# The adapter's four batches rewritten as one stream of 23 slots

## The reference, cut to what matters

```python
enc, ca = ctx[:, :73], ctx[:, 73:]                  # 77 rows of 96; the last 4 are tokens
hs      = mha(x @ Wq, enc @ Wk, enc @ Wv)           # text branch, 8 heads of 20
ca_q1   = einsum('btc,th->bch', ca, Wq_ca)[:, indices]   # 96 distinct rows, repeated to 512
ca_hs1  = mha(ca_q1, x, x)                          # token branch: softmax over 512 rows of x
ca_hs2  = mha(ca_hs1 @ Wq, ca @ Wk_ca, ca @ Wv_ca)  # softmax over 4 tokens
x       = (hs + ca_hs2) @ Wout + b_out + x
```

## Time and profile before

| | |
|---|---|
| runs | 1092.45, 1094.27, 1095.04 us; median 1094.27 |
| profiled execution, span | 1096.6 us, 2.3 over the median |
| PE, DVE, ACT, POOL busy | 93%, 64%, 55%, 32% of the span |
| mean granted TensorE clock | 0.964 |
| adapter | from 0 to about 215 us |

### The profile page before, as it was taken

One profiled execution on the slowest core, in us unless ns is written; L12 is line 12 of the kernel. 1 busy time (PEld: TensorE's weight loads), 2 busy tenths in 40 slices (PEclk: granted clock), 3 DMA queues, 4 the chain that ended last, 5 costly groups with the idle time before them and its releaser, 6 DMA issues.

```text
span 1096.6 us, 17611 instructions
## 1 busy us (share of the span) xinstructions
PE 1018.4 (93%) x6388; PEld 721.8 (66%) x6388; DVE 706.5 (64%) x1228; ACT 598.1 (55%) x1344; POOL 350.0 (32%) x461
## 2 busy tenths in 40 slices
PE   6788887799999999999999999999999989999998
PEld 3455553556666766666766666766656569999887
DVE  2544737377767467767367767377662879999563
ACT  2534434466677456677366676366662654555432
POOL 2303214133433224433233433133331023444220
PEclk9878988899999999999999999999999999999999
DMA  6700000000000000000000000000000240000000
GB/s 165 186 1 1 2 1 0 1 1 1 1 1 1 1 1 2 1 1 1 1 1 1 1 1 1 1 1 1 1 1 1 64 129 14 1 1 1 1 25 25
DMA packets 25319, 17.67 MB, mean 16 GB/s; under 512 B 8482, under 2 KB 24050, under 8 KB 25234
## 3 DMA queue, kind: packets, MB, share of 16 engines
q1 hardware_dynamic: 25234, 16.54, 5.8%
HBM read 11.29 MB, written 1.31 MB: 11 GB/s over the span
## 4 chain that ended last, share of the span: by engine, by line
PE 61%; DVE 10%; ACT 5%; issue 4%; POOL 1%; DMA 0%; SPq 0%; DVEq 0%; ACTq 0%; POOLq 0%
PE banks L415 12%; PE banks L402 11%; PE banks L388 10%; PE banks L422 4%; ACT sa_probs L505 3%; PE banks L224 3%; PE banks L226 2%; PE banks L227 2%; PE banks L225 2%; PE banks L1460 2%; PE banks L1752 2%; DVE sa_negmax L577 2%; DVE ca_top L1595 1%; DVE ca_probs L1600 1%; PE banks L232 1%
## 5 line engine op out<-in xcount | busy, mean ns | idle before, releaser
L645 POOL TENSOR_SCALAR sa_probs<-sa_probs,sa_inverse 128x512 f32<-128x512 f32 x320 | 217.6, 696 | 373.8 <-DVE sa_inverse L581 373.7
L505 ACT ACTIVATE sa_probs<-banks,sa_negmax 128x512 f32<-128x512 f32 x320 | 215.9, 685 | 163.2 <-DVE sa_negmax L577 163.1
L577 DVE TENSOR_REDUCE sa_negmax<-banks 128x2 f32<-128x1024 f32 x160 | 188.6, 1218 | 12.6 <-PE banks L388 9.9
L402 PE MATMUL banks<-ident,sa_probs 128*128 128x128 f32 x1280 | 175.1, 278 | 10.0 <-ACT sa_turned L516 5.7
L402 PEld LDWEIGHTS banks<-ident,sa_probs 128*128 128x128 f32 x1280 | 146.9, 142 | 55.9 <-issue 28.0
L586 DVE COPY sa_turned<-banks 128x512 f32<-128x512 f32 x160 | 110.1, 688 | 77.5 <-PE banks L402 77.5
L415 PE MATMUL banks<-sa_turned,sa_v 128*64 128x512 f32 x640 | 155.0, 605 | 0.0
L388 PE MATMUL banks<-sa_k_parts,sa_q_parts 64*128 64x512 f32 x960 | 134.4, 411 | 1.9 <-ACT sa_probs L505 1.9
L516 ACT COPY sa_turned<-banks 128x512 f32<-128x512 f32 x160 | 94.4, 590 | 31.7 <-PE banks L402 30.0
L388 PEld LDWEIGHTS banks<-sa_k_parts,sa_q_parts 64*128 64x128 f32 x960 | 84.8, 187 | 31.2 <-issue 14.6
L415 PEld LDWEIGHTS banks<-sa_turned,sa_v 128*64 128x64 f32 x640 | 38.7, 136 | 74.2 <-issue 73.0
(11 more groups left out here) (212 smaller groups left out, 1757.4 us busy)
## 6 DMA issues: line engine op xcount, KB each, us to landing
w_o<-in_L_xattn_wo SPq DMA_DIRECT2D x2, 800.0 KB, 6.4
out<-x SPq DMA_DIRECT2D x4, 320.0 KB, 2.4
w_q_t<-in_L_xattn_wq_t SPq DMA_DIRECT2D x1, 1120.0 KB, 11.2
fold_values<-ca_turned SPq DMA_DIRECT2D x5, 192.5 KB
x<-in_x SPq DMA_DIRECT2D x1, 960.0 KB, 6.0
fold_values<-ca_probs SPq DMA_DIRECT2D x4, 192.5 KB
ad_raw_main<-in_L_xattn_wq SPq DMA_DIRECT2D x1, 640.0 KB, 4.1
ad_raw_main<-in_L_xattn_wk SPq DMA_DIRECT2D x1, 640.0 KB, 6.2
```

The costliest lines, as they stand in the source:

```text
L402: last = pe.transpose(b_turn[e][:, q * P:(q + 1) * P], probs[:, j % 2, e, q, k * P:(k + 1) * P], ident[:])
L505: act.activation(probs[:, j % 2, e, q, :], b_scores[u % 2][:, e, :], ACT.Exp, bias=negmax[:, u % RING, e:e + 1], accum_out=total[:, u % RI ...
L577: dve.tensor_reduce(negmax[:, u % RING, :], b_scores[u % 2], AX_X, ALU.max, negate=True).then_inc(s_max.sem, 1)
L645: pool.tensor_scalar(probs[:, j % 2, e, q, :], probs[:, j % 2, e, q, :], inverse[:, u % RING, e:e + 1], 1.0, ALU.mult, ALU.mult).then_inc( ...
```

## The change

The batch loop becomes a loop over 23 slots. Slot s has head pair s of the token branch (16 of them, batch s // 4) and query tile u = s - 4 of the text branch. A tile's probabilities are turned one slot after its scores, its products follow two slots after, and its projection and update of x three slots after. The batch's token tail (second query projection, four-token scores and softmax, expansion) is spread over slots 4b+4 to 4b+6, so that it is there when tile 0 of that batch is projected.

- All transposes, the query projections, the expansion and one extra product share two PSUM banks (2 and 3) in a fixed order (`Turns`): each filling waits for the copy of the filling two before. Which engine copies is fixed by item.
- Contexts of all four batches are loaded by one DMA (and tokens by one), and their token queries, keys and values are projected ahead of slot 0. Keys are spread into block-diagonal form by POOL with a mask, two batches' buffers deep, in place of DVE copies.
- The token values are multiplied by `wo` once (`token_outputs`, slot 2). Each tile's projection then has a third matmul, of the expanded probabilities (K = 32) with these folded values, and the accumulation onto all heads (L975) is gone.
- Products, their copy, the projection and the update of one tile use one bank (4).
- The weight splits are cut into 12 chunks, one in each of slots 3 to 14. The raw buffers lie over tiles that are loaded only later: the five large loads (`last`, 3.68 MB) are issued after the last chunk's remainder.
- x_pad, x_t and q_t get a second buffer; x_pad is cleared by DVE instead of POOL.

What follows is the new code's core; the helpers that are left out do the same operations on the same shapes as before, one tile or head pair at a time.

```diff
-class Raw:
-    def __init__(self, ctx, nc, name):
-        self.main = ctx.enter_context(nc.sbuf_tensor(name + "main", [P, INNER], F32))
-        self.tail = ctx.enter_context(nc.sbuf_tensor(name + "tail", [3 * DT, INNER], F32))
...
+class Turns:
+    BANKS = (2, 3)
...
+    def of_slot(s, units, delta):
+        b, k = divmod(s, QT)
+        u = s - delta
+        out = [("x", 0, g) for g in range(G)] if s == 0 else []
+        out += [("probs1", s - 1, e) for e in range(2)] if 1 <= s <= units else []
+        out += [("probs", u - 1, g) for g in range(G)] if 1 <= u <= units else []
+        if k == 0 and b < B:
+            out += [("queries", b, 0)]
+        if k == 1 and b + 1 < B:
+            out += [("x", b + 1, 0)]
+        if k == 2 and 1 <= b <= B:
+            out += [("expanded", b - 1, 0)]
+        if k == 2 and b == 0:
+            out += [("token_outputs", 0, 0)]
+        if k == 2 and b + 1 < B:
+            out += [("x", b + 1, 1)]
+        if k == 3 and b < B:
+            out += [("queries", b, 1)]
+        return out
...
+        return banks[Turns.BANKS[self.items.index(item) % 2]]
+    def wait_free(self, pe, item):
+        n = self.items.index(item) - 2
...
+def adapter(nc, t, x, ident, ctx_t, banks, splits, raws, later, last, next_ln):
...
+        NU = B * QT
+        DELTA = 4
+        SLOTS = NU + DELTA + 3
+        HT = H0 * NCA
...
+        b_s1, b_small, b_token, b_out = banks.pair(0), banks.pair(5), banks[7], banks[4]
...
+            def project_out(u):
+                b, q = divmod(u, QT)
+                rows = slice(b * HT, (b + 1) * HT)
+                pe.wait_ge(s_heads.sem, s_heads.at(u, 0))
+                if q == 0:
+                    ring.wait_copied(pe, ("expanded", b, 0))
+                for g in range(G):
+                    pe.matmul(b_out[:, OUT:OUT + D], heads[:, u % 2, g, :], wo[:, g, :], start=(g == 0), stop=False)
+                pe.matmul(b_out[:, OUT:OUT + D], probs2x[rows, q * P:(q + 1) * P], v2_out[rows, :], start=False, stop=True).then_inc(s_o.sem, 1)
...
+            for s in range(SLOTS):
+                b, k = divmod(s, QT)
+                u = s - DELTA
+                if s < NU:
+                    scores1(s)
+                if 1 <= s <= NU:
+                    turn_probs1(s - 1, 0)
+                    turn_probs1(s - 1, 1)
+                if k == 1 and 1 <= b <= B:
+                    project_hs1(b - 1)
+                if 0 <= u - 3 < NU:
+                    project_out(u - 3)
+                if 0 <= u < NU:
+                    scores(u)
+                if 0 <= u - 1 < NU:
+                    turn_probs(u - 1, 0)
+                    turn_probs(u - 1, 1)
+                if 0 <= u - 2 < NU:
+                    products(u - 2)
+                if k == 0 and b < B:
+                    project_queries(b, 0)
+                if k == 0 and 1 <= b <= B:
+                    products1(b - 1, 1)
+                if k == 1 and b + 1 < B:
+                    turn_x(b + 1, 0)
+                if k == 1 and 1 <= b <= B:
+                    scores2(b - 1)
+                if k == 2 and 1 <= b <= B:
+                    expand_probs2(b - 1)
+                if s == 2:
+                    token_outputs()
+                if k == 2 and b + 1 < B:
+                    turn_x(b + 1, 1)
+                if k == 2 and b < B:
+                    products1(b, 0)
+                if k == 3 and b < B:
+                    project_queries(b, 1)
+                if s == NU + 1:
+                    pe.wait_ge(s_exp1.sem, s_exp1.at(NU - 1, 1))
+                    next_ln.turn(pe, 0, ident, banks[0:2], lambda i: None)
...
+            for s in range(SLOTS):
+                b, k = divmod(s, QT)
+                u = s - DELTA
+                if 0 <= u - 3 < NU:
+                    copy_heads(u - 3)
+                if k == 1 and 1 <= b <= B:
+                    copy_hs1(b - 1)
+                if 1 <= s <= NU:
+                    copy_turned1(s - 1, 0)
+                    copy_turned1(s - 1, 1)
+                if k == 2 and 1 <= b <= B:
+                    exp2(b - 1)
+                if s < NU:
+                    exp1(s, 0)
+                    exp1(s, 1)
+                if k == 1 and 1 <= b <= B:
+                    copy_q2(b - 1)
+                if 0 <= u - 1 < NU:
+                    copy_turned(u - 1)
+                if 0 <= u < NU:
+                    exp(u)
+                if s in chunks:
+                    i, c = chunks[s]
+                    act.wait_ge(s_raw, 16 * Split.LOADS * len(splits))
+                    splits[i][1].round(act, raws[i], columns(c), s_rounded.sem)
+                if k == 0 and b < B:
+                    copy_queries(b, 0)
+                if k == 1 and b + 1 < B:
+                    copy_x(b + 1)
+                if k == 2 and 1 <= b <= B:
+                    copy_expanded(b - 1)
+                if s == 2:
+                    item = ("token_outputs", 0, 0)
+                    ring.wait_made(act, item)
+                    act.copy(v2_out[:], ring.bank(banks, item)[:, 0:D]).then_inc(ring.s_act, 1)
+                if k == 3 and b < B:
+                    copy_queries(b, 1)
+                if s == NU + 1:
+                    act.wait_ge(s_later, 16 * len(later))
+                    next_ln.scale_and_round(act, 0, banks[0:2], lambda eng: None)
...
+            for s in range(SLOTS):
+                b, k = divmod(s, QT)
+                u = s - DELTA
+                if k == 2 and 1 <= b <= B:
+                    shift2(b - 1)
+                if s == 1:
+                    dve.wait_ge(s_xrest, 16)
+                if k == 1 and b + 1 < B:
+                    pad_x(b + 1)
+                if s < NU:
+                    max1(s)
+                if k == 2 and 1 <= b <= B:
+                    finish2(b - 1)
+                if 0 <= u - 3 < NU:
+                    update(u - 3)
+                if 0 <= u < NU:
+                    shift(u)
+                if s < NU:
+                    inverses1(s)
+                if 0 <= u - 1 < NU:
+                    copy_turned(u - 1)
+                if 0 <= u < NU:
+                    inverses(u)
+                if k == 2 and b + 1 < B:
+                    copy_x(b + 1)
+                if s in chunks:
+                    i, c = chunks[s]
+                    dve.wait_ge(s_rounded.sem, s_rounded.at(s - 3, 1))
+                    splits[i][1].rest(dve, raws[i], columns(c), s_rest.sem)
+                if s == NU - 2:
+                    dve.wait_ge(s_x.sem, s_x.at(QT - 1, 0))
+                    next_ln.statistics(dve, 0)
+                if s == NU - 1:
+                    next_ln.standardize(dve, 0)
+                if s == NU + 1:
+                    next_ln.remainder(dve, 0, lambda eng: None)
...
+            def spread_keys(b):
+                if b >= 2:
+                    pool.wait_ge(s_s.sem, s_s.at((b - 2) * QT + QT - 1, 0))
+                pool.tensor_tensor(k_diag[:, b % 2, :, :, :], each(k_all[:, :, b * SE:(b + 1) * SE]).broadcast_to([P, G, HG, SE]),
...
+            for s in range(SLOTS):
+                b, k = divmod(s, QT)
+                u = s - DELTA
+                if s < NU:
+                    pool.wait_ge(s_inv1.sem, s_inv1.at(s, 0))
+                    for e in range(2):
+                        i = (2 * s + e) % 4
+                        pool.tensor_scalar(probs1[:, i, :], probs1[:, i, :], inverse1[:, i:i + 1], 1.0, ALU.mult, ALU.mult).then_inc(s_norm1.sem, 1)
+                if 0 <= u < NU:
+                    pr = probs[:, u % 2, :, :, :].rearrange("p g h k -> p (g h) k")
+                    pool.wait_ge(s_inv.sem, s_inv.at(u, 0))
+                    pool.tensor_tensor(pr, pr, inverse[:, u % 2, :].unsqueeze(2).broadcast_to([P, H0, SE]), ALU.mult).then_inc(s_norm.sem, 1)
+                if k == 2 and 1 <= b < B:
+                    spread_keys(b)
+                if s == 3:
+                    pool.wait_ge(s_wo, 16 * N_WO)
+                if k == 3 and b < B:
+                    add_bias(b)
+                if s == NU - 2:
+                    next_ln.deviations(pool, 0)
...
-            adapter(nc, t, x, ident, ctx_t, banks, [(w("wq1"), wa), (w("wk1"), wb), (w("wv1"), wc)], later, ln1)
+            last = [(w_o1[:], pairs(w("wo1"))), (w_k2[:], w("wk2")), (wq_t[:], pairs(w("wq2_t"))), (w_o2[:], pairs(w("wo2"))), (w_v2[:], w("wv2"))]
+            tail = early.enter_context(nc.sbuf_tensor("raw_tail", [3 * DT, INNER], F32))
+            raws = [Overlaid(main[:].rearrange("p j d -> p (j d)")[:, 0:INNER], rest[:]) for main, rest in ((wq_t, w_k2), (w_o2, w_v2), (w_o1, tail))]
+            adapter(nc, t, x, ident, ctx_t, banks, [(w("wq1"), wa), (w("wk1"), wb), (w("wv1"), wc)], raws, later, last, ln1)
```

More of the change, by code:

```diff
@@ new lines, in turn_x, with project_queries @@
+                ring.wait_free(pe, item)
+                for q in range(QT):
+                    last = pe.transpose(ring.bank(banks, item)[:, q * P:(q + 1) * P],
```

(43 more changed lines are left out.)

755 lines of the change are left out of this document (335 added, 420 removed).

## The result

The changed kernel takes **1059.4 us** (median of 4 runs, 1055.6 to 1063.1), the kernel before 1093.4 beside it (4 runs, 1092.0 to 1095.0): ratio 0.9693, 95% interval 0.9657 to 0.9729. That is 34 us less where the prediction said 53 less; 1059 lies inside the wide range (1028 to 1062), 3 us from its upper end, and outside the forecast's own range (1036 to 1048). The profiled execution took 1055.8 us with a span of 1054.0.

A forecast was written before the change was run, and what follows sets the result against it. The adapter was taken as bound by a chain of handoffs, PE's work close behind. Self-attention would start at 163.1 us against 216.4, 53.3 less: span 1043.3, minus 2.3 to the median, 1041; own range 1036 to 1048, wide range 1028 to 1062.

The forecast's parts named there:

- full slots: Slots 7 to 15, both branches running: PE work 7.9, 8.4 with clock 0.94, plus 0.5 for DVE waits: 8.9 us each.
- rival 2: Full slots take 10.7 us, from a clock of 0.77 to 0.8 or DVE waits delaying the turn banks; 1057, chance 0.24.
- rival 1: Full density: PE never idles, clock stays 1.0, nothing collides; 7.9 us a slot, 1032, chance 0.16.
- The collision of DVE and POOL: In the stream, DVE's weight remainders wait for POOL's tile scaling: 1.0 us a slot on DVE, PE sees 0.5.
- slots 4 to 6: Stream filling up, ahead of the full slots: 6.2, 7.0 and 7.7 us, ending at 51.3.
- The prologue: Before slot 0: small weights, token queries, keys and DVE copies; first token scores at 13.9 us, 6.1 sooner.
- Slots 0 to 3: Token branch alone, 4.2 us from one exponential to the next; ends at 30.4 us.
- The tail: Slot 16 to self-attention's first matmul: tiles alone about 5 us a slot, norm 3 in slot 17; first matmul at 163.1.
- The last loads: Five loads (3.68 MB) starting near 123 us end at 160 at 100 GB/s, so they are hidden.
- the 2 us counted in slot 4: ACT waits in slot 3 for all twelve raw loads, landing near 32.5 us, delaying the first query scores 2 us.
- Rivals 3 and 4: Stream: in-order queue stalls, 12.5 us a slot, 1073, chance 0.08; or turn-bank waits closing into a ring, 1138, chance 0.03.
- Rival 4: Turn-bank waits form a ring, both chains run one after the other, 16.5 us a slot with handoffs; 1138, chance 0.03.

The follow-up runs named there:

- rest_early: The changed kernel with each chunk's two DVE weight remainders moved to the next slot, behind the update of x; 1049.1 us, ratio 0.9586.
- warm_start: The changed kernel with 8 useless identity matmuls on PE after the identity lands and 3 after x is turned; 1052.3 us, ratio 0.9637.
- tail_ln: The changed kernel with the next norm's five ACT operations laid one to a slot in slots 17 to 21, not all in 17; 1054.1 us, ratio 0.9645.
- combined2: combined with a semaphore for each weight's raw load, so ACT's rounding waits only for its own weight; 1036.2 us, ratio 0.9481.
- combined3: combined2 without the useless identity matmuls of the last four slots; 1044.2 us, ratio 0.9547.
- combined: The changed kernel with warm_start, rest_early and tail_ln together, plus useless identity matmuls in slots 19 to 22; 1045.4 us, ratio 0.9542.
- the change again: The changed kernel unaltered, rerun as yardstick beside the kernel before; 1056.4 us, ratio 0.9661.

## Why the prediction was right, and where it missed

The restructuring did what the prediction said, and the time lies in its wide range. That it comes so near is in part luck: misses of 21.5 us at the filling and the emptying stand against 8.4 too much in the full slots. The nearest figure on its list, rival 2's 1057, had a slower slot as its reason, and that did not come.

- **The restructuring and its size.** That the adapter was bound by handoffs, and that a stream would fill PE, held: 40.2 us fewer ahead of self-attention of the 53.3 forecast. What follows takes 877.8 us against 880.2, with the same instructions.
- **The full slots, 8.9 forecast, 8.0 measured.** The term that failed is the clock: it stayed at 1.00, where 0.94 was taken (0.5 a slot). PE's work, 7.9 by the rows of before, is 7.6 (68.15 us busy in nine slots, and 7.55 in rest_early), so the sum was 0.3 too high. The rest of the 8.0 is 0.4 of idle time, nearly all of which went away in rest_early: the 0.5 taken for DVE's remainders was about right. That 8.0 looks like rival 1's 7.9 is therefore chance; rival 1 as a whole (1032) fell, because its full clock did not hold at the ends.
- **The collision of DVE and POOL was real, and put in the wrong place.** Remainders of 1334 ns against 483, and one of 2757, agree with the Trainium skill, "SBUF — State Buffer", section "Who interferes with whom", in that an instruction waits for a whole one of the other engine; the longest waited for two in a row. The measured cost a slot on DVE, 1.0, is the one forecast. But the remainders hurt most before the full slots, in slots 4 to 6, where 3.8 us more than forecast were spent: in rest_early slots 4 to 6 take 20.1, against 20.9 forecast. What the prediction left out is that the remainders also stand ahead of the next slot's maximum, and that the wait of 2.07 us which they cause was followed by the half clock. rest_early is worth some 8 us (0.9586 against 0.9661) where the prediction had 4 for the collision alone.
- **The prologue, 13.9 forecast, 18.8 measured.** The failing step took durations from rows of a PE that had been working (L889's 1.25) for a stretch in which it had barely begun. The sign was in the profile of before, where L862's first eight took 5.46 us and those of the third batch 3.60:

  ```profile
  14.63 5.46 PE L862 MATMUL banks<-ad_x_t,ad_wq 128*128 128x512 f32 x8 [1.18 <-DMA ad_wq<-in_L_xattn_Wq]
  ```

  warm_start, with 14.15, shows that little else was wrong. Slots 0 to 3 are 1.3 over for the same reason: slot 0 takes 5.6 us (18.77 to 24.38), the next three 3.9 to 4.2.
- **The tail, 31.7 forecast, 43.2 measured: the largest miss.** The norm's operations were counted as 3 us in slot 17, but not as a wait of PE behind the copy of the heads (3.20), and nothing was added for the clock, though tiles alone leave PE idle every few us. tail_ln took 6.6 off in its profile. But no profile has this stretch under 36.7 us, so 5 of the 11.5 have another cause. "Tiles alone" is the step that was wrong: slots 16 to 18 also carry the last batch's token tail, 3.5 us of PE's time by its rows (0.84, 1.13, 0.51, 1.02) and 0.75 of waiting, which the sum has at nothing; slot 16 takes 6.2 us from tile scores to tile scores at the full clock, where 5.3 were forecast. How many of the 5 us this makes no run here tells. The Trainium skill, "TensorE: Matmul & The Clock Gate", section "Part 1: The HAM clock gate", ties the half clock to idleness, and at this end the runs agree: work that computes nothing is worth 8 us there (combined2 against combined3). In the stream they agree in part only, as the last section shows.
- **The last loads** were hidden, as forecast: they moved at 214 GB/s in slots 16 and 17, and no wait names them. The raw loads cost nothing in the change's profile, where the 2 us counted in slot 4 did not come, and 8 us in combined's.
- **Rivals 3 and 4** never came: no ring of waits at the turn banks, and no full slot over 9 us. (Rival 4's two chains add up to 16.6, with nothing for handoffs; its verdict doesn't hang on it.)

## What to carry to other kernels

Where a pipeline is filled so that PE hardly waits, its price per turn can be summed from the instructions' rows and came out within 5% here; the filling and emptying can't, and there the half clock and operations of the next stage in a shared queue cost more than the waits one counts. Once a stretch gets faster, read again every wait that it used to hide: here one semaphore over twelve loads went from nothing to 8 us. Elementwise work with both inputs in SBUF belongs beside an idle POOL, and not ahead of an operation for which the next slot waits, and cheap matmuls are worth trying wherever PE idles before dense work, but not where a load sets the time.

## What the runs showed of the hardware

- The granted clock fell to 0.50 with PE busy 8.00 of 8.00 us (64 to 72 us, the change again). It had stood still for 2.10 us ahead. After the same 2.07 us of idle time in slot 5 one profile shows half rate (1.93 for the scores) and another (tail_ln) the full one (1.10): for the same instructions it comes or not from run to run. The two bunches of times, some 6 us apart, go with it as far as the two profiles of the change show, one of each bunch: the slower one spends 8 us more ahead of slot 8, all of it around such stretches.
- Even a busy PE didn't always keep it: combined2's and combined3's instructions are the same up to the tail, but in the one the clock is 0.50 from 13 to 20 us and the first scores come at 16.82, in the other it is 1.00 there and 0.50 from 20 to 30. PE was busy for 10.43 of the 11 us ahead of that first stretch. What sets off these stretches stays open.
- In the first 19 us the clock column says 1.00 while matmuls take twice their later time (2.02 against 1.10), and in the profile of the change again it says so still from 24.4 to 36.6 us, with scores of 2.02 at 24.39 and 29.80. Durations of one instruction form are the safer reading there.
